# The second key head's projection moved to the start of a two-layer attention kernel, and the splits and copies around the first normalisation reordered

## What is computed

```python
x = x + _L0_xattn_ref(_layernorm(x, axis=-1), ctx_4096, ctx_4096, mask, Wq, Wk, Wv, Wo)

q = apply_rope((query @ Wq).reshape(b, t, h, d))
k = apply_rope((key @ Wk).reshape(b, t, kv_h, d))
v = (value @ Wv).reshape(b, t, kv_h, d)
logits = MAX_ATTN_VAL * jnp.tanh(ATTN_MULT * einsum('btkgd,bTkd->bkgtT', q, k) / MAX_ATTN_VAL)
weights = jax.nn.softmax(jnp.where(m, logits, -1e+30), axis=-1)
attn = einsum('bkgtT,bTkd->btkgd', weights, v).reshape(b, t, h * d) @ Wo
```

## Time and profile before

| | us |
|---|---|
| median of three runs | 885.11 (885.04 to 886.01) |
| the profiled execution, its time | 885.15 |
| its span in the profile | 883.4 |
| PE busy | 848.6 |
| DVE / ACT / POOL busy | 485.4 / 350.9 / 303.0 |
| PE's first matmul starts | 6.38 |

### The profile page before, as it was taken

How to read it: one execution, slowest core, us unless ns; L and a number is a source line. 1 busy time by engine, 2 the same in 40 slices (tenths; PEclk the granted TensorE clock), 3 DMA queues, 4 the chain that set the end, 5 groups by cost and what they waited for, 6 DMA issues and landing times.

```text
span 883.4 us, 12370 instructions
## 1 busy us (share of the span) xinstructions
PE 848.6 (96%) x4758; PEld 701.9 (79%) x4758; DVE 485.4 (55%) x876; ACT 350.9 (40%) x827; POOL 303.0 (34%) x232
## 2 busy tenths in 40 slices
PE   5999999999999999999999999979989999999998
PEld 4788887887887887877877777749978888888776
DVE  5856654755654655555565547452135544555674
ACT  5343222223123123023113233546576666766542
POOL 3386525624525525525535330010031111211132
PEclk9999999999999999999999999989999999999999
DMA  8122211311212211211212131010020110210002
GB/s 286 42 79 79 72 37 53 92 37 48 72 37 72 72 37 49 73 37 49 72 37 81 50 90 36 17 36 1 13 72 10 43 33 25 85 59 1 1 1 96
DMA packets 24891, 48.15 MB, mean 55 GB/s; under 512 B 3584, under 2 KB 4736, under 8 KB 24704
## 3 DMA queue, kind: packets, MB, share of 16 engines
q1 hardware_dynamic: 24400, 47.22, 17.9%
q10 hardware_dynamic: 432, 0.14, 0.1%
HBM read 45.12 MB, written 2.23 MB: 54 GB/s over the span
## 4 chain that ended last, share of the span: by engine, by line
PE 81%; ACT 9%; DVE 5%; DMA 2%; issue 2%; POOL 1%; SPq 0%; POOLq 0%; ACTq 0%; DVEq 0%
PE PB L1084 21%; PE PB L1086 20%; PE PB L1085 20%; PE PB L1242 5%; PE PB L1147 3%; PE PB L1173 2%; PE PB L1091 2%; ACT Eb L832 2%; PE PB L1257 2%; PE PB L1274 2%; DMA stage<-in_wo 2%; DVE Ol L1055 1%; ACT Oh L703 1%; PE PB L1157 1%; DVE sm L1037 1%
## 5 line engine op out<-in xcount | busy, mean ns | idle before, releaser
L662 POOL TENSOR_TENSOR qb<-qb,arena 128x512 f32<-128x512 f32 x64 | 82.6, 1291 | 128.2 <-DVE arena L942 127.8
L864 DVE TENSOR_TENSOR xs<-xs,PB 128x512 f32<-128x512 f32 x112 | 76.2, 686 | 91.7 <-PE PB L1086 84.2
L1085 PE MATMUL PB<-WOl,Oh 128*128 128x512 f32 x256 | 99.9, 390 | 0.0
L1084 PE MATMUL PB<-WOh,Oh 128*128 128x512 f32 x256 | 99.9, 390 | 0.0
L1086 PE MATMUL PB<-WOh,Ol 128*128 128x512 f32 x256 | 99.8, 390 | 0.0
L703 ACT ACTIVATE Oh<-PB 128x512 fp32r<-128x512 f32 (+2 forms) x160 | 69.1, 468 | 58.0 <-PE PB L1173 39.8
L653 POOL TENSOR_TENSOR WQl<-stage,WQh 128x512 fp32r<-128x512 f32 x38 | 48.8, 1287 | 98.9 <-ACT WQh L703 87.7
L1084 PE MATMUL PB<-xTh,WQh 128*128 128x512 f32 x192 | 77.4, 403 | 1.8 <-DVE xTl L916 1.8
L1085 PE MATMUL PB<-xTl,WQh 128*128 128x512 f32 x192 | 75.4, 393 | 0.0
L1086 PE MATMUL PB<-xTh,WQl 128*128 128x512 f32 x192 | 75.4, 393 | 0.0
L973 DVE TENSOR_TENSOR Ol<-PB,Oh 128x512 fp32r<-128x512 f32 x64 | 39.8, 684 | 64.5 <-ACT Oh L703 64.5
(11 more groups left out here) (203 smaller groups left out, 2052.0 us busy)
## 6 DMA issues: line engine op xcount, KB each, us to landing
stage<-in_wq SPq DMA_DIRECT2D x44, 256.0 KB, 3.0
stage<-in_wo SPq DMA_DIRECT2D x44, 256.0 KB, 2.6
arena<-recs SPq DMA_DIRECT2D x32, 256.0 KB, 3.9
stage<-in_wk SPq DMA_DIRECT2D x14, 256.0 KB, 2.8
arena<-in_ctxT SPq DMA_DIRECT2D x8, 256.0 KB, 5.8
stage<-in_wv SPq DMA_DIRECT2D x8, 256.0 KB, 3.1
xs<-in_x SPq DMA_DIRECT2D x8, 256.0 KB, 6.3
out<-xs SPq DMA_DIRECT2D x8, 256.0 KB, 2.0
```

The costliest lines, as they stand in the source:

```text
L662: e.tensor_tensor(dst, dst, tmp, ALU.add).then_inc(s_radd)
L864: e.tensor_tensor(xs[:, i, :], xs[:, i, :], PB[b][:, :], ALU.add).then_inc(free[b])
L1084: e.matmul(dst, Ah, Bh, start=(k == 0), stop=False)
L1085: e.matmul(dst, Ah, Bl, start=False, stop=False)
```

## The change

The second key head's two tiles, `("k0", 1, 0)` and `("k0", 1, 1)`, move from units 0 and 1 to the head of the program: the first behind `mask_tables` and ahead of the first query tile, the second behind `("k0", 0, 1)`. Their weight `wk0[1]` is the first one loaded behind x, and is split into `more[2..3]`, which is free until the fourth output weight is split; the condition on that one names `("k0", 1, 1)`. The weight of the third key head is split in its place, once `("k0", 0, 1)` has been made.

The three value tiles stand ahead of the first `xn`, as do the splits of `wk0[1]` and `wq0[0]` and the first two value copies. The splits of `wq0[1]` and `wq0[2]` stand behind the four normalised tiles, and `("ctx", 1)` behind `("k0", 1, 0)`. The DMAs of the second half of the context and of the last four x tiles are issued later, behind the loads of `wq0[0]` to `wq0[2]`. With two tiles more in the head, the turn of the banks is another from `("q0", 0, 0)` to `("d0", 0)`.

```diff
--- before.py
+++ after.py
@@ -124,27 +124,34 @@
         step("load", "wv0", 0, c)
     for i in LO:
         step("x", i)
-    step("ctx_load", 1)
-    step("load", "wq0", 0)
+    step("load", "wk0", 1)
     split("wk0", 0)
     step("ctx", 0)
     for c in range(2):
         split("wv0", 0, c)
-    for i in HI:
-        step("x", i)
     for i in LO:
         step("stats", 0, i)
     step("rstd", 0, 0)
     ring.remove(3)
     stage("k0", 0, 0)
-    normed(0, LO, [lambda: split("wq0", 1), lambda: (step("v0_move", 0, 0), stage("v0", 0, 3)),
-                       lambda: (step("v0_move", 0, 1), split("wq0", 2))],
-           [lambda i=i: stage("v0", 0, i) for i in range(3)] + [lambda: split("wq0", 0)])
+    for i in range(3):
+        stage("v0", 0, i)
+    split("wk0", 1)
+    step("ctx_load", 1)
+    for i in HI:
+        step("x", i)
+    step("v0_move", 0, 0)
+    split("wq0", 0)
+    step("v0_move", 0, 1)
+    normed(0, LO, [None, lambda: stage("v0", 0, 3)])
     tile("many", bank=3)
     step("mask_tables")
-    step("ctx", 1)
     for i in range(2, 4):
         step("v0_move", 0, i)
+    split("wq0", 1)
+    split("wq0", 2)
+    stage("k0", 1, 0)
+    step("ctx", 1)
     q0(0, 0)
     split("wq0", 3)
     for i in HI:
@@ -154,7 +161,8 @@
     q0(0, 2)
     q0(0, 3)
     stage("k0", 0, 1)
-    split("wk0", 1)
+    split("wk0", 2)
+    stage("k0", 1, 1)
     normed(0, HI, [lambda i=i: v0(0, i) for i in range(5, 8)], [lambda: v0(0, 4)])
 
     ring.remove(2)
@@ -186,7 +194,7 @@
         queries(3)
         outputs(2)
         j, hf = u // 2 + 1, u % 2
-        if j < 8:
+        if 1 < j < 8:
             stage("k0", j, hf)
             if hf and j + 1 < 8:
                 split("wk0", j + 1)
@@ -540,10 +548,14 @@
 
             return {"l0": ("e0", 14 + i // 4, i % 4), "ffn": ("delta", i), "l1": ("e1", 24 + i)}[when]
 
+        def wk0_home(j):
+
+            return wo_home[3] if j == 1 else (WKh[:, :], WKl[:, :])
+
         def split_home(kind, *k):
 
             if kind == "wk0":
-                return a["wk0"][k[0]], 512, WKh[:, :], WKl[:, :]
+                return a["wk0"][k[0]], 512, *wk0_home(k[0])
             if kind == "wv0":
                 cols = slice(512 * k[1], 512 * k[1] + 512)
                 return a["wv0"][k[0]][:, cols], 512, WVh[:, cols], WVl[:, cols]
@@ -563,7 +575,7 @@
         def split_after(kind, *k):
 
             if kind == "wk0":
-                return ("k0", k[0] - 1, 1) if k[0] else None
+                return ("k0", k[0] - 1 - (k[0] == 2), 1) if k[0] >= 2 else None
             if kind == "wv0":
                 return ("v0", k[0] - 1, 7) if k[0] else None
             if kind == "wq0":
@@ -571,7 +583,7 @@
                 return ("q0", h // 4 * 2 + 1, h % 4) if h >= 0 else None
             if kind == "wo0":
                 h = k[0] - 4
-                return ("e0", h // 4 * 2 + 1, 3) if h >= 0 else None
+                return ("e0", h // 4 * 2 + 1, 3) if h >= 0 else ("k0", 1, 1) if k[0] == 3 else None
             if kind == "wk1":
                 return {(0, 0): ("k0", 7, 1), (1, 0): ("q0", 15, 0), (2, 0): ("q0", 15, 1), (0, 1): ("k1", 0, 0, 1),
                         (1, 1): ("k1", 0, 1, 1), (2, 1): ("k1", 1, 1, 1)}[k]
@@ -1099,11 +1111,12 @@
                 if kind == "k0":
                     j, hf = k
                     cols = slice(512 * hf, 512 * hf + 512)
+                    hi, lo = wk0_home(j)
                     pe.wait_ge(*lo_ready("wk0", j))
                     for c in range(4):
                         w = slice(c * 128, c * 128 + 128)
                         pe.wait_ge(s_clo, 4 * hf + c + 1)
-                        last = thrice(PB[b][:, :], c, 4, WKh[:, w], WKl[:, w], cTh[:, c, cols], cTl[:, c, cols])
+                        last = thrice(PB[b][:, :], c, 4, hi[:, w], lo[:, w], cTh[:, c, cols], cTl[:, c, cols])
                     last.then_inc(full[b])
                 elif kind == "q0":
                     u, n = k
```

## The result

The changed kernel takes 888.68 us (median of 12 runs, 886.65 to 892.62), the kernel before beside it 885.62 (12 runs, 882.94 to 886.68). The ratio is 1.0045 with a 95% interval of 1.0032 to 1.0057: slower by 3.1 us by the medians, where 2.0 less was forecast. The ratio is taken over all the runs and is not the quotient of the two medians; by it the loss is 4.0 us (2.8 to 5.0). The time lies outside the forecast's range of 881.8 to 885.0. The profiled execution took 890.79 us for a span of 889.0.

The account below looks back on a forecast made before the run. TensorE, with work for 848.6 of 883.4 us, was taken as the bound, through idle holes and a slow clock. Gain 3.34 less 0.24 and 1.08 gives 2.02 us: 885.15 - 2.02 = 883.1, range 881.8 to 885.0.

Parts of the forecast that it names:

- The early part: Head up to the filler: first xn at 15.69 us, added splits and copies free, 0.3 us of ScalarE cover left.
- The filler fills: Key tile ahead of the first query tile runs 20.5 to 23.3 us at full clock, where TensorE had idled.
- the late filler: Rival, chance 0.06: low half of wk0[1] comes 2.4 us late, filler runs 22.9 to 25.7; total 885.5 us.
- x landing earlier: Rival, chance 0.10: with four ctx transfers gone from behind x, rstd comes up to 0.5 us earlier; total 882.6.
- What is late next: Fourth query tile waits some 1.35 us for wq0[3]'s low half, set by VectorE, starting at 32.85 instead of 33.38.
- The clock there: At the fourth query tile: the 1.35 us wait lies between full tiles, so the clock stays full.
- The rival of one fall: Chance 0.12: the clock falls once in the head, TensorE or VectorE's chain loses 1.70 us; total 884.8.
- To the first scores: From the fourth query tile to `("b0", 0)`: 2.72 + 5.62 + 7.83 us, giving 49.02 instead of 46.74.
- Paid back at `("b0", 1)`: TensorE comes at 65.41 but goes on at 65.65, behind the last query addition: 0.24 us lost.
- Paid back at `("d0", 0)`: TensorE waits 82.6 to 83.65 for bank 1, late through the DRAM round trip: 1.08 us lost.
- The rival by which this cover was not needed: Chance 0.13: bank 1 or the DRAM round trip is not late, only 0.24 us paid back; total 882.0.
- The 4.6 us of holes: Before `("q0", 0, 3)`: TensorE idle 1.17 and 1.75 us plus slow clock 1.70; 3.34 us was to be gained.

Follow-up runs that it names:

- Experiment 1: Changed kernel with the split of wq0[3] ahead of the first query tile (887.29 us), with mask tables in PSUM (886.11), and with both edits (886.01).
- no filler: Changed kernel with both key tiles back in units 0 and 1, the moved copies, splits and loads kept: 885.61 us (1.0006).
- the copy: Kernel before, unchanged, run again for its scatter and a second profile: 885.14 us (0.9998).
- experiment 2: Changed kernel with the loads of wq0[8] to wq0[10] behind the first norm's DMAs: 886.05 us; with mask tables in PSUM as well, 885.12.
- experiment 5: Both kernels run again unchanged, for second profiles and times at equal mean clock: kernel before 885.14 us, changed kernel 888.16.
- experiment 4: Changed kernel, tables in PSUM, loads late, wq0[3] split earlier: first tile in front 883.11 us, both tiles 883.67, neither 885.58.
- the split ahead: Changed kernel with the split of wq0[3] ahead of the filler's rotary steps, plus both cures: one tile in front 883.11 us, both tiles 883.67.
- both cures: Changed kernel with mask tables in PSUM and the loads of wq0[8] to wq0[10] behind the first norm's DMAs: 885.12 us (0.9995).

## Why the prediction was wrong, step by step

- **The early part.** First `xn` at 15.86 (15.69 forecast), the idle time of ScalarE before it 0.23 where 0.3 of cover was left: right. The 0.17 came with x, not from the splits and copies. The splits and copies cost nothing.
- **The filler fills.** 20.67 to 23.54 at full clock, forecast 20.5 to 23.3: right. The rivals of the late filler and of x landing earlier (10.12 against 9.94) are out.
- **What is late next.** The chain was right (filler's rotary step, ctx subtractions, `("q0", 0, 0)`, addition, split), its prices were not. The filler's rotary step was put at 23.5 and began at 24.85, since the mask tables, which the sum had at nothing, took 2.0 us more; the subtractions were put at 2.4 between starts and took 3.5 (26.96 to 30.48). So the rotary steps of `("q0", 0, 0)` began at 30.48 instead of 28.05, 2.43 late, and `("q0", 0, 3)` at 35.27 instead of 32.85, 2.42 late. The failed step is taking durations of DVE from rows in which POOL was idle, and using them for a place where the change sets POOL's work beside them. Experiment 1 shows the first term alone (with the tables in PSUM the wait for W is 1.10 shorter). The second goes with the number of POOL instructions beside the subtractions: 2.49 without any (no filler), 3.59 with one, 4.68 with two.
- **The clock there.** The 1.35 us wait that was thought harmless was 3.37 long, and behind it the tile took 4.16 in place of 2.72: 1.44 lost. The rival of one fall had it, at 1.70, with a chance of 0.12, and a half clock between 20 and 36 was among the signs of being wrong; it began at 34.7. And the 1.70 that the fall in the kernel before was said to cost, and the filler to win back, was 1.60 by the copy (23.22 from the first query matmul to b0(0) against 21.62), and is not paid in every execution of the kernel before.
- **To the first scores.** 49.02 forecast, 52.50 measured: 2.42 + 1.44, less 0.38 that the stretch of value tiles took up.
- **Paid back at `("b0", 1)`.** 16.64 us from b0(0), forecast 16.63: right.
- **Paid back at `("d0", 0)`.** PE arrives at 84.99 and SP issues at 74.47, both as forecast plus the 3.48 of delay (84.98 and 74.45). The DRAM round trip, taken as 7.24, took 7.85, and DVE's rotary steps came 0.63 later than forecast with it. 1.87 lost instead of 1.08. In the copy, with the same loads ahead of it, the round trip took 7.12, the wait was 0.47 instead of 1.19, and b0(2) came 36.12 us behind b0(0), where 36.06 was forecast. So the forecast of this term was sound and its miss here is scatter; experiment 2 removes the wait. The rival by which this cover was not needed is out.
- **The sum.** 85.08 forecast for `("b0", 2)`; 3.48 + 0.01 + 0.79 later is 89.36, as measured. The whole miss of 4.28 at this place is thus 2.42 of DVE's durations, 1.44 of the clock behind them and 0.79 of the round trip, less 0.38. The 3.2 us more of the profiled span come in the feed-forward part and are scatter (experiment 5).
- **What was not asked at all:** what bounds the beginning if every wait that was named is taken away. The 4.6 us of holes in front of `("q0", 0, 3)` were read as if PE could have them all. The table in experiment 4 says that DVE's chain takes the same time whether PE waits for W or not. By it the kernel before, at full clock, had some 0.4 us between PE and DVE's floor; that is an estimate, 18.41 less 18.0.

## What to carry to other kernels

A filler for an idle engine has to be priced on the engines that finish its work too: here 2.8 us of matmuls brought 2.1 us of VectorE steps, and the stretch behind them is one where VectorE has no gap. When a change puts GpSimd work beside VectorE work, list which of the VectorE instructions read only SBUF, and price those anew; here moving one small operand to PSUM took 2.0 us out of two instructions. And before a slow clock in one profile is counted as something to win, look at a second execution of the same kernel. Before two profiles are compared to tenths of a microsecond, find the first event that the change can't touch and count from it.

## What the runs showed that was not expected

Instructions of 128x64 on VectorE, 0.20 and 0.23 us alone, took 1.24 and 1.26 beside 128x512 instructions of GpSimd with both inputs in SBUF, and 0.23 and 0.22 beside the same with an operand in PSUM. Rotary multiplications, with one input from PSUM, stayed at 0.67 to 0.69 in all rows read. Four 128x512 subtractions in SBUF grew by 1.10 with one GpSimd instruction beside them, by 2.2 with two, by 2.35 with three, of which the first was already running when they began.

None of the versions is faster than the kernel before by more than can be measured. The two with a filler, the split ahead and both cures have medians 1.3 to 1.8 us below it and intervals that hold 1; whether the 0.4 and 1.1 us that their profiles show at b0(2), counted from the first transposes, are there in the mean stays open.
